# Slot list of the experts made on chip by TensorE from one-hot rows, in place of 128 GpSimd scatters into DRAM

## What is computed

```python
scores_BSN = jnp.einsum('bsd,nd->bsn', x, Wr) + br
w_BSN = jax.nn.softmax(scores_BSN, axis=-1)
_, idx_BSK = jax.lax.top_k(scores_BSN + biases_N[None, None, :], K)      # K = 2 of 8 experts
...
y_NMD = jnp.einsum('nmh,nhd->nmd', jax.nn.silu(a_NMH) * b_NMH, Wl2) + bl2[:, None, :]
y_MD = jnp.einsum('mn,nmd->md', ew_MN, y_NMD)                            # ew: the two gates of a token
...
x = x + s * silu(y)                                                      # s: the attention output
```

## Time and profile before

| | us |
|---|---|
| median of 3 runs | 1495.42 (1495.07 to 1499.51) |
| span of the profiled execution | 1494.3 |
| PE busy | 1361.6 (91%) |
| DVE busy | 1280.2 (86%) |
| ACT busy | 823.8 (55%) |
| POOL busy | 804.3 (54%) |
| 128 scatters, POOL busy | 132.8 |

### The profile page before, as it was taken

The page is one execution under the profiler, slowest core; times in us unless marked ns, Lnnn a source line. Parts: engine busy times, 40 slices in busy tenths (PEclk is TensorE's granted clock), DMA queues, the critical chain, the costliest instruction groups (busy, mean ns, idle before and its releaser), DMA issues.

```text
span 1494.3 us, 35841 instructions
## 1 busy us (share of the span) xinstructions
PE 1361.6 (91%) x13687; PEld 1085.4 (73%) x13688; DVE 1280.2 (86%) x1504; ACT 823.8 (55%) x1889; POOL 804.3 (54%) x566
## 2 busy tenths in 40 slices
PE   5998899984799999999999998999999978797988
PEld 4864565653688888888888886887888856675766
DVE  7837655556699999999999999999999999999961
ACT  2547687864445555555555554554555436574655
POOL 1001477773587766767666877768686651311111
PEclk9999999985999999999999999999999988898999
DMA  7933366564957676768677666767777679999897
GB/s 231 352 130 101 115 203 208 166 222 158 287 122 224 170 232 161 222 161 235 183 204 214 168 179 160 214 159 201 196 190 221 133 178 232 250 218 246 217 246 148
DMA packets 203481, 293.52 MB, mean 196 GB/s; under 512 B 24833, under 2 KB 160261, under 8 KB 203123
## 3 DMA queue, kind: packets, MB, share of 16 engines
q0 software_dynamic: 65792, 146.59, 38.5%
q1 hardware_dynamic: 134915, 144.84, 33.6%
q10 hardware_dynamic: 2672, 0.83, 0.2%
HBM read 182.83 MB, written 117.74 MB: 201 GB/s over the span
## 4 chain that ended last, share of the span: by engine, by line
DVE 48%; DMA 8%; PE 8%; issue 6%; SPq 5%; POOL 0%; ACT 0%; POOLq 0%; DVEq 0%
DVE gslope L1647 11%; DVE parts L1643 11%; DVE parts L1603 8%; DMA band<-band_rows 7%; DVE expert_mem L1569 5%; PE pB L1480 3%; DVE parts L1615 3%; SPq L1121 2%; DVE parts L1619 2%; DVE parts L1622 1%; PE pA L1465 1%; PE pY L1490 1%; DVE gslope L1700 1%; SPq L1115 1%; DVE wgt L1708 1%
## 5 line engine op out<-in xcount | busy, mean ns | idle before, releaser
L1175 POOL DMA_INDIRECT moe_rows<-expert_mem,token_of x142 | 324.9, 2288 | 76.2 <-issue 47.9
L1446 PE MATMUL pA<-xsT,expert_mem 128*128 128x256 f32 x1136 | 264.5, 387 | 22.6 <-DMA expert_mem<-in_w_l 15.5
L1156 POOL DMA_INDIRECT expert_mem<-xn_rows,token_of x142 | 222.3, 1566 | 96.8 <-issue 74.2
L1452 PE MATMUL pY<-expert_mem 128*128 x1136 | 265.7, 387 | 0.0
L1446 PEld LDWEIGHTS pA<-xsT,expert_mem 128*128 128x128 f32 x1136 | 220.3, 195 | 55.9 <-issue 20.0
L1446 PE MATMUL pB<-xsT,expert_mem 128*128 128x256 f32 x1136 | 256.8, 379 | 0.0
L1452 PEld LDWEIGHTS pY<-expert_mem 128*128 128x128 f32 x1136 | 211.1, 191 | 42.3 <-issue 16.2
L1446 PEld LDWEIGHTS pB<-xsT,expert_mem 128*128 128x128 f32 x1136 | 215.8, 190 | 29.3
L1643 DVE SCALAR_TENSOR_TENSOR parts<-pos_pair,prob 128x768 f32<-128x768 f32 x256 | 228.0, 953 | 1.1
L1647 DVE TENSOR_REDUCE gslope<-parts 128x256 f32<-128x3072 f32 x64 | 214.7, 3354 | 2.2
L1297 ACT ACTIVATE expert_mem<-pA,b1sel 128x256 f32<-128x256 f32 x284 | 111.3, 474 | 135.3 <-issue 93.2
(11 more groups left out here) (197 smaller groups left out, 2036.3 us busy)
## 6 DMA issues: line engine op xcount, KB each, us to landing
expert_mem<-in_w_l POOLq DMA_DIRECT2D x71, 1024.0 KB, 7.0
band<-band_rows SPq DMA_DIRECT2D x256, 96.0 KB, 5.5
S_rows<-stage SPq DMA_DIRECT2D x64, 376.0 KB
band_rows<-wgt SPq DMA_DIRECT2D x12, 1536.0 KB, 7.1
pos_pair<-pos_rows SPq DMA_DIRECT2D x28, 384.0 KB, 7.7
xn_rows<-stage SPq DMA_DIRECT2D x16, 512.0 KB, 5.4
v_rows<-stage SPq DMA_DIRECT2D x16, 512.0 KB, 4.2
moe_rows<-zeros POOLq DMA_DIRECT2D x4, 2048.0 KB
```

The source lines that it names most:

```text
L1156: nc.gpsimd.indirect_dma_start(out=xs[:, u, s], out_offset=None, in_=dram["xn"], in_offset=bass.IndirectOffsetOnAxis(ap=keep["inv"][:, 2 * ...
L1175: nc.gpsimd.indirect_dma_start(out=dram["moe"], out_offset=bass.IndirectOffsetOnAxis(ap=keep["inv"][:, 2 * n + s:2 * n + s + 1], axis=0), ...
L1446: mm = nc.tensor.matmul(dst[:, c], w1[:, 1 - u, k, o * HID + c * P:o * HID + (c + 1) * P], xsT[:, k], start=(k == 0), stop=(k == KC - 1))
L1452: mm = nc.tensor.matmul(pY[:, s], hid[:, h, c, s * P:(s + 1) * P], w2[:, c, ds(e * D, D)], start=False, stop=(s == 1 and c == HC - 1))
```

## The change

The DRAM list, the 128 scatters, the list's initial store and its reload are taken out. In their place:

- DVE makes exact one-hot rows in bf16 in 32 parts of 4 columns (`hot_part`): for each of the 4 x 128 choices of a part a row of 128 that has a one at the slot's low part, and a row of 142 that has a one at its high part, once times the lane number and once times the tile number. Each part has four DVE instructions.
- PE multiplies them (`place_part`): per part 4 bf16 products of 128x128 by 128x284, all 128 summed into one PSUM region (`pList`).
- Three parts are made per step from step 3 on (LIST_FROM = 3), so parts 0 to 29 in steps 3 to 12 and parts 30 and 31 in step 13. One part stands before `slopes_of_k` and two after it on DVE; on PE they stand before `head_scores(n, 2)`, before `head_scores(n, 3)` and at the end of the step. Two buffers alternate, so part b waits for PE to have used part b - 2.
- In step 15 DVE makes `token_of` out of PSUM with six small instructions (`tokens_of_slots`), ahead of `offset_bias(14, 0)`. The two instructions that read the reloaded list go.
- `find_slots` loses its last instruction; DVE copies two small constants more; POOL makes two iotas for them in place of one. `clear_moe` now only waits for `pos_ready`, with no scatters ahead of it.

```diff
+LIST_PART = 4
+LIST_PARTS = LISTED // LIST_PART
+PARTS_EACH = 3
...
         @block.gpsimd
...
-            pool.dma_start(dram["list"].rearrange("(p n) o -> p (n o)", p=P), spare_i[:]).then_inc(list_set, 16)
...
-            pool.wait_ge(list_set, 16)
-            pool.wait_ge(list_rows, 1)
-            def scatter(some):
-                for c in some:
-                    nc.gpsimd.indirect_dma_start(
-                        out=dram["list"], out_offset=bass.IndirectOffsetOnAxis(ap=list_row[:, c:c + 1], axis=0),
-                        in_=token_i[:, c:c + 1], in_offset=None).then_inc(scattered, 16)
...
             for q in range(4):
-                scatter(range(q * LISTED // 4, min((q + 1) * LISTED // 4, LISTED - 8)))
                 clear_moe(q)
-            scatter(range(LISTED - 8, LISTED))
...
-            pool.wait_ge(scattered, 16 * LISTED)
-            pool.dma_start(spare_i[:], dram["list"].rearrange("(p n) o -> p (n o)", p=P)).then_inc(list_loaded, 16)
...
         @block.tensor
+            def place_part(b):
+                if b < 0 or b >= LIST_PARTS:
+                    return
+                pe.wait_ge(hot_ready, b + 1)
+                for i in range(LIST_PART):
+                    mm = nc.tensor.matmul(pList, low_hot[b % 2][:, i], high_hot[b % 2][:, i].rearrange("p f n -> p (f n)"),
+                                          start=(b == 0 and i == 0), stop=(b == LIST_PARTS - 1 and i == LIST_PART - 1))
+                mm.then_inc(hot_used, 1)
...
                     offsets(n - 1, 1)
+                place_part((n - LIST_FROM) * PARTS_EACH)
                 head_scores(n, 2)
...
+                place_part((n - LIST_FROM) * PARTS_EACH + 1)
                 head_scores(n, 3)
...
+                place_part((n - LIST_FROM) * PARTS_EACH + 2)
...
         @block.vector
+            def hot_part(b):
+                if b < 0 or b >= LIST_PARTS:
+                    return
+                low, high, cols = low_hot[b % 2], high_hot[b % 2], slice(b * LIST_PART, (b + 1) * LIST_PART)
+                tile = b * LIST_PART % TILES
+                if b >= 2:
+                    dve.wait_ge(hot_used, b - 1)
+                V.tensor_tensor(low, place[:, None, 0:LOW].broadcast_to([P, LIST_PART, LOW]),
+                                slot_low[:, cols].unsqueeze(2).broadcast_to([P, LIST_PART, LOW]), ALU.is_equal)
+                chain(V.tensor_tensor(high[:, :, 1], place[:, None, :].broadcast_to([P, LIST_PART, HIGH]),
+                                      slot_high[:, cols].unsqueeze(2).broadcast_to([P, LIST_PART, HIGH]), ALU.is_equal))
+                chain(V.tensor_scalar(high[:, :, 0], high[:, :, 1], lane[:, 0:1], None, ALU.mult))
+                V.tensor_tensor(high[:, :, 1], high[:, :, 1], place[:, tile:tile + LIST_PART].unsqueeze(2).broadcast_to([P, LIST_PART, HIGH]),
+                                ALU.mult).then_inc(hot_ready, 1)
+
+            def tokens_of_slots():
+                dve.wait_ge(hot_used, LIST_PARTS)
+                V.tensor_copy(token_f[:], pList[:, 0:HIGH])
+                chain(V.tensor_scalar(list_f[:], pList[:, 0:HIGH], 0.0, None, ALU.is_equal))
+                chain(V.tensor_tensor(list_f[:], list_f[:], spare_i[:], ALU.mult))
+                chain(V.scalar_tensor_tensor(token_f[:], pList[:, HIGH:], float(P), token_f[:], ALU.mult, ALU.add))
+                chain(V.tensor_tensor(list_f[:], list_f[:], token_f[:], ALU.add))
+                V.tensor_scalar(keep["inv"][:], list_f[:], -1.0, None, ALU.add)
...
+                hot_part((n - LIST_FROM) * PARTS_EACH)
                 if n + 2 < STEPS:
                     slopes_of_k(n + 2)
+                for i in range(1, PARTS_EACH):
+                    hot_part((n - LIST_FROM) * PARTS_EACH + i)
+                if n == STEPS - 1:
+                    tokens_of_slots()
...
-            dve.wait_ge(list_loaded, 16)
-            chain(V.tensor_copy(list_f[:], spare_i[:]))
-            V.tensor_scalar(keep["inv"][:], list_f[:], float(TOKENS), None, ALU.add)
```

More of the change, by code:

```diff
@@ L181, in front_block @@
         wqk = sb("wqk", [P, KC, 2 * D])
-        wvr = sb("wvr", [P, KC, D + EXPERTS])
+        HOT_F = LIST_PART * HIGH
+        wvr_mem = sb("wvr", [P, max(KC * (D + EXPERTS), HOT_F)])
+        wvr = wvr_mem[:, 0:KC * (D + EXPERTS)].rearrange("p (k n) -> p k n", k=KC)
+        LOW_F = LIST_PART * LOW // 2
+        low_hot = [stage[:, u * LOW_F:(u + 1) * LOW_F].bitcast(BF16).rearrange("p (i n) -> p i n", n=LOW) for u in range(2)]
+        high_hot = [mem.bitcast(BF16).rearrange("p (i f n) -> p i f n", f=2, n=HIGH)
+                    for mem in (stage[:, 2 * LOW_F:2 * LOW_F + HOT_F], wvr_mem[:, 0:HOT_F])]
+        assert 2 * LOW_F + HOT_F <= 4 * GROUP_F - SX_F
         br_bc = sb("br_bc", [P, EXPERTS])
@@ L209, in front_block @@
         list_f = sb("list_f", [P, HIGH])
+        token_f = sb("token_f", [P, HIGH])
+        place_i = sb("place_i", [P, HIGH], I32)
+        place = sb("place", [P, HIGH], BF16)
         spare_i = sb("spare_i", [P, HIGH], I32)
-        token_i = sb("token_i", [P, TOPK * TILES], I32)
+        lane_i = sb("lane_i", [P, 1], I32)
+        lane = sb("lane", [P, 1])
         slot_i = sb("slot_i", [P, TOPK, TILES], U32)
         high_part = sb("high_part", [P, TOPK, TILES], U32)
-        slot_low = sb("slot_low", [P, TOPK * TILES])
-        slot_high = sb("slot_high", [P, TOPK * TILES])
-        list_row = high_part[:].rearrange("p k t -> p (k t)")
+        slot_low = sb("slot_low", [P, TOPK * TILES], BF16)
+        slot_high = sb("slot_high", [P, TOPK * TILES], BF16)
         dw_w = sb("dw_w", [P, KC, 3])
@@ L239, in front_block @@
         pOff = ps("pOff", [P, 512])
-        pCount = ps("pCount", [P, 2 * EXPERTS])
+        pCount = ps("pCount", [P, 512])
+        pList = pCount[:, 512 - 2 * HIGH:]
         weights_in = sem("weights_in")
@@ L287, in front_block @@
         prefix_ready = sem("prefix_ready")
-        list_set = sem("list_set")
         list_rows = sem("list_rows")
-        scattered = sem("scattered")
-        list_loaded = sem("list_loaded")
+        hot_ready = sem("hot_ready")
+        hot_used = sem("hot_used")
         TAIL = VROWS - TOKENS - REACH
@@ L296, in front_block @@
         ROUTE_WEIGHTS = WEIGHTS + 16 * 5
-        CONSTS = 8
+        CONSTS = 9
+        LIST_FROM = COUNT_AT + 2
         def qcol(n):
@@ L849, in find_slots @@
                 chain(V.tensor_scalar(slot_i[:], slot_i[:], LOW - 1, None, ALU.bitwise_and))
-                chain(V.tensor_copy(slot_low[:], slot_i[:].rearrange("p k t -> p (k t)")))
-                V.scalar_tensor_tensor(list_row, slot_low[:], float(HIGH), slot_high[:],
-                                       ALU.mult, ALU.add).then_inc(list_rows, 1)
+                ins = V.tensor_copy(slot_low[:], slot_i[:].rearrange("p k t -> p (k t)"))
+                chain(ins)
+                dve.sem_inc(list_rows, 1)
+            def hot_part(b):
[20 more added lines that the diff above has]
+                V.tensor_scalar(keep["inv"][:], list_f[:], -1.0, None, ALU.add)
             def experts_of_pairs():
@@ L892, in _ @@
             V.tensor_copy(tile_row[:], keep["tile_exp"][:])
+            V.tensor_copy(place[:], place_i[:])
+            V.tensor_copy(lane[:], lane_i[:])
             chain(V.tensor_copy(base[:], base_i[:]))
@@ L1744, in build @@
         "moe": nc.dram_tensor("moe_rows", [TOKENS + SPARE, D], F32).ap(),
-        "list": nc.dram_tensor("slot_list", [SLOTS, 1], I32).ap(),
         "bias": nc.dram_tensor("bias_parts", [NB, EXPERTS, 2 * D], BF16).ap(),
```

7 lines of the change are left out of this document (3 added, 4 removed).

## The result

The changed kernel takes 1546.7 us (median of 4 runs, 1544.1 to 1559.95) against 1495.24 us of the kernel before beside it: ratio 1.035, 95% interval 1.031 to 1.040. That is 51 us slower; 45, so 1540 us, had been forecast. The profiled execution has a span of 1542.4 us, 48.1 above the 1494.3 of before.

A forecast was written before the change was run, and what follows sets the result against it. PE was taken to bound the steps, with DVE becoming the bound after the change. Stretch +39.4, `tokens_of_slots` +1.6 and `find_slots` -0.3 gave +40.7; with +4 for the clock, 1494.3 + 45 = 1539, as median 1540; range 1515 to 1560.

The forecast's parts named there:

- A part is 2.46 us.: DVE's four new instructions per part: 2.46 us, bounds 1.6 and 2.9; times 32 that is 79 us.
- Rival (b): Two-input bf16 instructions on DVE cost half per column; a part is 1.6 us, PE sets the pace, 1514 us; chance 0.10.
- The ring closes after 18.1 us.: Steps' loop of DVE's `offset_bias` and PE's offsets, each waiting for the other: 18.1 us a turn, against 14.5 before.
- Stretch +39.4, and +4 for the clock.: Steps 3 to 13: 198.9 against 159.5 us; TensorE's lower clock in three of eleven steps adds 4.
- A product 0.13 us, 1.6 us a step.: PE's bf16 products in the steps: 0.13 us each, 12 a step, 17 us in all, covered by DVE.
- `tokens_of_slots` +1.6.: Step 15: six DVE instructions of 142 columns ahead of an `offset_bias` PE waits for, +1.6 us.
- -0.3 from `find_slots`.: Step 2: dropping the last instruction of `find_slots` saves about 0.3 us.
- `positions` faster with POOL quiet, taken as 0.: DVE's four-instruction `positions` row might gain at most 0.3 us a step, 3 us in all; taken as 0.
- The second block as long as before.: From the barrier to the end: unchanged at 1131 us, only starting later, about 405 in place of 363.7.
- The path gains nothing from that: 0.: Removing 128 scatters, a store and a load from POOL saves 0, the list being some 12 us early.
- I take 0, because nearly all other waits are semaphore waits between engines: Earlier clears and missing scatter packets in the steps: bounded at -4.3 to +4.3 us by PE's "issue" gaps, taken as 0.
- Rival (c), not slower, 0.05.: DVE's idle time swallows the parts, PE's the products; no change (0.03) or faster (0.02), chance 0.05.

The follow-up runs named there:

- pe_alone: `no_list` plus PE's 128 products in their places, on the rows of parts 0 and 1 alone, sum unused: 1507.74 us, 1.008 of the kernel before.
- dve_alone: `no_list` plus DVE's 32 parts in their places, unused, with no products on PE: 1547.27 us, 1.036 of the kernel before.
- after_again: The changed kernel run once more, unaltered, in a later set: 1548.38 us, 1.035 of the kernel before.
- third_later: The changed kernel with the third part of a step moved on DVE to between the two `offset_bias`: 1530.08 us, 0.930 of the kernel before.
- no_list: The kernel before without scatters, parts or products; slots take tokens by a fixed rule, so the second block works on wrong tokens: 1498.99 us, ratio 1.002.
- no_list_paced: `no_list` with the four clears of 2 MB split into sixteen of 0.5 MB: 1489.03 us; the kernel before beside it 1650.14.
- warm: The changed kernel with five f32 products of zeros added on PE ahead of `offsets(n - 1, 1)` in steps 3 to 12: 1550.14 us.
- spread: The changed kernel with the first part ahead of `positions`, the third between the two `offset_bias`, and clears in sixteen pieces: 1509.92 us.
- dve_only: The changed kernel with DVE's parts but no PE products, the list made by the 128 scatters as before: 1665.33 us, 1.010 of the kernel before.
- both_lists2: The changed kernel with the 128 scatters, store and reload put back on POOL, second block using PE's list: 1666.14 us, 1.009 of the kernel before.

## Why the prediction was right, and where it wasn't

The sign, the size and the mechanism held: the bound of the steps moved from PE to DVE. Point by point:

- *A part is 2.46 us.* 2.45 measured (244.22 to 246.67 in the timeline), with 685, 745, 371 and 751 ns where 0.69, 0.75, 0.36 and 0.75 had been named. Rival (b), half the price per column for two-input bf16, is out: 568 columns in bf16 cost what the f32 line gives. The one-input multiply came out at the lower of its two bounds (0.37 us, and 0.41 from its start to the next one's). So of the two rules of the Trainium skill the second held, that of Vector Engine (DVE) Microarchitecture Reference, section 5.1, which reports the single rate for an instruction with two inputs that reads one element again and again (16 times there, a row of 128 or 142 here). The trace agrees: 685 ns for 512 columns of bf16, where the f32 row has 692.
- *The ring closes after 18.1 us.* 17.97 at full clock. PE's gap ahead of `offsets(n, 1)` was put at 1.6 and is 1.53, the one ahead of the second part at 0.6 and is 0.61.
- *Stretch +39.4, and +4 for the clock.* +43.3. The clock fell in four turns of the first ten, for 5 us in all; the full-clock turns were a little shorter than forecast, and step 13 a little longer. The sum itself has a slip: 181 + 1.8 + 15.7 is 198.5 and not 198.9, so +39.0. The edge instructions stand in steps 9 and 10, one later than it says. That the clock would fall in some steps was right; the number of them, three of eleven, was a guess that came out near. Three of the four falls stand behind idle times that also occur in turns at full clock, and one behind a stop of 1.62 us with "issue", which had no place in the forecast. What decides between them isn't shown.
- *A product 0.13 us, 1.6 us a step.* 0.147 (four in 0.59 us, from 250.40 to 250.99), and 1.47 us a step in `pe_alone`, 0.122 each; the 0.13 lies between. That they are covered is shown by PE's 1.5 us of waiting behind them, in nine turns; 48.3 + 8.8 against 49.4 fits.
- *`tokens_of_slots` +1.6.* It takes 1.7 us, but the way from the stretch to the second block stayed at 41.5. In the last step the clock came back sooner than before (offsets at 394.33 take 1.57). That the one paid for the other isn't shown.
- *-0.3 from `find_slots`.* Not seen: the stretch begins 0.2 us later than before (162.84 against 162.65).
- *`positions` faster with POOL quiet, taken as 0.* The row fell from 342 to 316 ns, 0.1 us a step, in DVE's part of the ring; the 0.3 a step named as the most was too much.
- *The second block as long as before.* It was 4.6 us longer in this execution. In other profiles without scatters it ran 1124 to 1132 us (`dve_alone` 1123.8, `after_again` 1130.7, `third_later` 1131.1, `no_list` 1131.6, `pe_alone` 1132.4). `after_again` is the same kernel, so the 4.6 us are the spread of executions and not the change. The total of 51 in place of 45 owes 4.6 to it, which no term of the sum held.
- *"The path gains nothing from that: 0."* As a number this was right where the kernel before takes 1495: `no_list` is level with it. As a reason it was wrong. That the list was 12 us early only shows that nobody waited for the list; it doesn't show that the scatters' traffic was free. Without it and with the clears in pieces the steps fall to 13.5 us, and the kernel without any list to 1489. The step that failed is the one on the clears and the scatter packets: "I take 0, because nearly all other waits are semaphore waits between engines". It looked in the right place, PE's "issue" gaps, but bounded their change by 4.3 us either way. In `no_list` they are 9.3 us in the stretch, 5.0 more than before, and the lower clock behind them comes on top; in `no_list_paced` they are 2.0. The clears moved ahead by a queue that had become empty, and PE stopped at DMA share 1.0. The collisions cost `no_list` 10 us against `no_list_paced` (of another set). That what the missing scatters gave back was hidden in them fits the plain steps, but isn't shown by a run. In the changed kernel PE is no longer the bound, so DVE's ring covers what the removal does to PE; one such stop is left (1.62 us). So the 0 did the forecast no harm, but not for the reason given. That `no_list` came out level is luck, two effects that nearly cancel.
- *Rival (c), not slower, 0.05.* This is the point on which the prediction was narrow. It argued from one trace. On two other chips the kernel before takes 1646.5 and 1650.1, and there every kernel without scatters is faster than it: `third_later` by 7.0% (ratio 0.925 to 0.934), `warm` by 6.1% (0.935 to 0.942). So the sign of the change depends on the chip, and the forecast holds only for those where the kernel before takes 1495. The changed kernel itself didn't run there, but these two are its nearest variants. Nothing in the trace of before showed this.

Is there a version that beats both? `spread` beats the changed kernel by 37 us, and the kernel before by 8.5% (0.911 to 0.918) where that takes 1650. Where the kernel before takes 1495, `spread` wasn't run; its 1509.9 of the other set would be about 1% slower. DVE's 79 us of one-hot rows don't fit into the 66 us of idle time that it had, and an order alone can't change that.

## What to carry to other kernels

Work that moves to an engine with idle time costs nothing only if the idle time lies where the work can stand. Here 79 us of work met 66 us of waits that belonged to a ring between two engines, and the same work cost 49 us in one order and about 21 (`spread` against `no_list_paced`: 1509.9 - 1489.0) in another. The two differ in their clears as well; with the clears of 2 MB in both, the better order of `third_later` cost 31 (1530.1 - 1499.0). When a queue is emptied, ask what stood behind it: the clears that the scatters had delayed went out sooner, and fell where they stopped PE. And a transfer that nobody waits for can still hold up the engines, on some chips by 100 us or more; small scattered writes to DRAM are worth a run on a second chip before a comparison is believed.

## What the runs showed of the hardware that was not expected

- 128 scatters of 128 four-byte values held up all engines but POOL on two chips: ten waits of ACT, of up to 34.7 and 29.8 us, with DMA share 0.02 and 0 GB/s in the window shown, 118 us (`dve_only` against `dve_alone`, 1665.3 - 1547.3, on different chips) and 116 us (`both_lists2` against `warm`, on one chip) in all. On two other occasions the same instructions did nothing of the kind. What tells the chips apart, and what the engines waited for, stays open.
- With the DMA engines at share 1.0 for some 8 us behind a 2 MB clear, PE stopped inside a row of 64 products for 1.56 to 3.33 us with "issue" as the reason (`no_list`); the same bytes in sixteen pieces took 10 us less in all. The changed kernel has one such stop of 1.62 us (253.40), at DMA share 1.02. The stop doesn't need a clear: the kernel before has one of 1.49 us (236.37), 30 us behind its last clear, at share 1.01. Whether PE's instructions came late wasn't tried.
- With the scatters running PE took 14.25 us for a step that took 13.52 without them, both at full clock and without idle time.
- Granted clock: idle times of 0.62 and 1.53 us were followed by offsets at full clock in one turn (272.94) and mostly at 1.2 GHz in another (291.20, granted clock 0.53), so the idle time just ahead doesn't decide. Single gaps of 3.36 and 4.27 us (`dve_alone`) were followed by the lower level both times. More idle time on PE (`dve_alone`) made each turn longer than in the changed kernel, in which PE had more to do.
